# One unrolled phase for two attention layers and a dispatch, in place of two phases one after the other

## The chip, the cores and the metric

The kernel runs on one core of one Trainium2 chip. The metric is the device time of one execution in microseconds (us), as the median of several runs. PE is TensorE's matmul row, PEld its weight loads, DVE is VectorE, ACT is ScalarE, POOL is GpSimd, SP is SyncE. PEclk is the TensorE clock that was granted, as a share of full speed.

## The reference

The input is 256 images of 128 channels and 7x7 = 49 places. Six layers follow one another. The change touches the second and the third, and the gate of the fourth (cut from the reference):

```python
def _L1_conv_ref(x, gn_scale, gn_bias, wq, bq, wk, bk, wv, bv, wp, bp):
    h_ = group_norm(x, gn_scale, gn_bias)            # 32 groups of 4 channels, over channels and places
    q, k, v = conv1x1(h_, wq, bq), conv1x1(h_, wk, bk), conv1x1(h_, wv, bv)
    attn = jax.nn.softmax(einsum('bci,bcj->bij', q, k) * c ** -0.5, axis=-1)
    return x + conv1x1(einsum('bij,bcj->bci', attn, v), wp, bp)

def _L2_attn_ref(x):                                 # no weights: a normed token is query, key and value
    return einsum('bnm,bmd->bnd', jax.nn.softmax(einsum('bnd,bmd->bnm', x, x), axis=-1), x)

x = _L1_conv_ref(x, ...)
t = _to_tokens(x)                                    # (256 * 49 tokens) x 128
t = t + _L2_attn_ref(_ln_t(t))
t = t + _L2_ffn_ref(_ln_t(t), ...)                   # 8 experts, the 2 best of a token by its 8 scores
```

The expert layer is computed only for the two experts that a token chose. For that the kernel first sorts: it norms each token, computes its eight scores, picks two, and writes the token's row to a place in the region of each of the two experts in DRAM. This is the dispatch.

## The kernel before

`X` holds all of x on chip, 128 channels on partitions and 256 x 49 places along the row. Work goes by groups of 8 images (`GI`; a group is 392 columns, `T`), 32 groups (`NG`). Two images share the partitions of a score tile: one on rows 0 to 48, one on rows 64 to 112, so 113 rows (`R`). The program is a row of phases, each closed by a barrier of all engines: `heads_phase` (layer 0), `single_phase` (the convolution-style layer), `token_dispatch_phase` (token attention and the dispatch), `blocks_phase` (experts of layer 2), `combine_phase`, `scales_dispatch_phase` (layer 3's attention and its dispatch in one phase, 3 tiles a chunk), `blocks_phase`, `final_phase`.

Inside a phase each engine runs its own list in order, and counters (semaphores) hold it until another engine has done its part. The lists are staggered by hand: in step s an engine works on group s+4 for one operation, on s-1 for another, so that the chains of several groups overlap.

`single_phase` (name `conv_`): per group, DVE sums over places (`sums`), PE turns sums into means of four channels, DVE subtracts (`centre`), ACT squares, DVE sums (`squares`), PE, ACT `rstd`, DVE `norm` into `xn`; PE makes queries and keys, ACT writes them out with bias; PE makes values (`tokens`, with wv and wp multiplied into one matrix), DVE `v_out` copies them; PE scores, DVE maximum and subtraction (`shift`), ACT `expo`, DVE `total` and reciprocal, POOL multiplies (`probs`), PE transposes (`turn`), ACT writes that out in four pieces as a block-diagonal `pt` (`turned`), PE `values` over 113 rows, DVE `residual` into `X`. Steps 4 to 27 are a hardware loop.

`token_dispatch_phase` (name `d_`): the same attention without projections, `centre` as a matmul, all in unrolled code; `probs` on DVE. When the groups of a chunk of four 128-token tiles are through (25 chunks), `Dispatch` follows: PE `turn` (tile to rows, `xt`) and `logits`, DVE `stats`, ACT `rstd` and `norm` into `row`, DVE `scale`, `choose`, `count_up`, PE `positions`, DVE `place` and `weigh`, ACT `gate`, `names`, `second`. POOL does only `scatter`: for each tile two indirect DMAs (one for each chosen expert), 196 in all. SP loads and stores the expert weights that ACT and DVE split (`split_high`, `split_low`), and after `table` (DVE) writes pads behind each expert's rows.

Of the kernel before, what the change touches and what calls it, by code (L numbers as in the profile page):

```python
# [14 lines left out]
F32 = mybir.dt.float32  # L15
# [732 lines left out]
def single_phase(nc, sh, kind, weights=None):  # L748

    conv = kind == "conv"
    X, ident = sh.X, sh.ident
    LEAD = 4
    with ExitStack() as ctx:
        def sb(name, shape, dt=F32):
            return ctx.enter_context(nc.sbuf_tensor(f"{kind}_{name}", shape, dt))  # L760

        def ps(name, shape):
            return ctx.enter_context(nc.psum_tensor(f"{kind}_{name}", shape, F32))

        sem = ctx.enter_context(PhaseSemaphores(nc, kind))

        if conv:
            st, pjq, pjk = ps("st", [C, 512]), ps("pjq", [C, 512]), ps("pjk", [C, 512])
        else:
            cps = [ps(f"cen{i}", [C, 512]) for i in range(2)]  # L770
            st = ps("st", [C, 512])
        vps = ps("vps", [C, 4, C])
        sps, ptps, ops_ = ps("sps", [C, 512]), ps("ptps", [C, 512]), ps("ops", [C, 512])
        if conv:
            w, b_in = weights
            b_use = sb("b_use", [C, 4])
            csum, ssum = sb("csum", [C, GI]), sb("ssum", [C, GI])
            cen = [sb(f"cen{i}", [C, T]) for i in range(2)]
            qt, kt = sb("qt", [C, T]), sb("kt", [C, T])
            wvt, wvp = sb("wvt", [C, C]), sb("wvp", [C, C])  # L780
        sq = sb("sq", [C, T])
        rs = sb("rs", [C, GI if conv else T])
        xn = [sb(f"xn{i}", [C, GI, B1]) for i in range(2)]
        vt = [sb(f"vt{i}", [R, 4, C]) for i in range(4)]
        sc = sb("sc", [R, PAIRS, N])
        pr = [sb(f"pr{i}", [R, PAIRS, B1]) for i in range(2)]
        mx, sm = sb("mx", [R, PAIRS]), sb("sm", [R, PAIRS])
        rc = [sb(f"rc{i}", [R, PAIRS]) for i in range(2)]
        pt = [sb(f"pt{i}", [C, 2, 2, 2, N]) for i in range(2)]

        wready, bmm, zeroed = sem("weights_ready"), sem("bias_products"), sem("zeroed")
        csum_done, mean_done, cen_done, sq_done, ssum_done = sem("csum"), sem("mean"), sem("centred"), sem("squared"), sem("ssum")
        var_done, ln_done, rs_done, xn_done = sem("variance"), sem("logvar"), sem("rstd"), sem("normed")
        q_mm, k_mm, q_done, k_done, v_mm, v_done = sem("q_mm"), sem("k_mm"), sem("q_out"), sem("k_out"), sem("v_mm"), sem("v_out")
        wv_turned, wv_out, wvp_mm = sem("wv_turned"), sem("wv_out"), sem("wvp_mm")
        s_mm, max_done, sub_done, exp_done = sem("s_mm"), sem("maxed"), sem("shifted"), sem("exped")
        sum_done, rec_done, prob_done = sem("summed"), sem("recip"), sem("probs")
        t_mm, t_done, pv_mm, res_done = sem("t_mm"), sem("t_out"), sem("pv_mm"), sem("residual")

        block = ctx.enter_context(nc.Block())  # L800

        def images(ap):
            return ap.rearrange("c (b n) -> c b n", n=N)

        @block.tensor
        def _(pe):
            if conv:

                for m in range(3):
                    last = pe.matmul(sps[:, m:m + 1], w[:, m * C:(m + 1) * C], b_in[:, 5:6], start=(m == 0), stop=True,  # L810
                                     skip_group_check=True)
                last.then_inc(bmm, 1)

                pe.wait_ge(wready, 2)
                pe.matmul(sps[:, 3:4], w[:, 3 * C:4 * C], b_use[:, 2:3], start=True, stop=True,
                          skip_group_check=True).then_inc(bmm, 1)
                pe.transpose(ptps[:, 0:C], w[:, 2 * C:3 * C], ident[:, :]).then_inc(wv_turned, 1)
                pe.wait_ge(wv_out, 1)
                pe.matmul(ops_[:, 0:C], wvt[:, :], w[:, 3 * C:4 * C], start=True, stop=True).then_inc(wvp_mm, 1)
                pe.wait_ge(wready, 5)  # L820
            pe.wait_ge(zeroed, 6)

            def mean(at):
                g = at.g
                if not at.exists():
                    return
                if conv:
                    if due(g - 1):
                        pe.wait_ge(ln_done, g - 1)
                    pe.wait_ge(csum_done, g + 1)  # L830
                    pe.matmul(st[:, 0:GI], sh.group_w[:, :], csum[:, :], start=True, stop=True).then_inc(mean_done, 1)
                else:
                    if due(g - 1):
                        pe.wait_ge(xn_done, g - 1)
                    pe.matmul(cps[at.r % 2][:, 0:T], sh.centre_w[:, :], X[:, cols(g)], start=True, stop=True).then_inc(mean_done, 1)

            def var(at):
                g = at.g
                if not at.exists():
                    return  # L840
                if conv:
                    pe.wait_ge(cen_done, g + 2 if at.ahead(1).exists() else NG)
                    pe.wait_ge(ssum_done, g + 1)
                    pe.matmul(st[:, 0:GI], sh.group_w[:, :], ssum[:, :], start=True, stop=True).then_inc(var_done, 1)
                else:
                    pe.wait_ge(sq_done, g + 1)
                    if due(g):
                        pe.wait_ge(ln_done, g)
                    pe.matmul(st[:, 0:T], sh.mean_w[:, :], sq[:, :], start=True, stop=True).then_inc(var_done, 1)

            def queries(at):
                g = at.g
                if not at.exists() or not conv:
                    return
                x = xn[at.r % 2][:, :, 0:N]
                pe.wait_ge(xn_done, g + 1)
                if due(g):
                    pe.wait_ge(q_done, g)
                pe.matmul(pjq[:, 0:T], w[:, 0:C], x, start=True, stop=True).then_inc(q_mm, 1)
                if due(g):  # L860
                    pe.wait_ge(k_done, g)
                pe.matmul(pjk[:, 0:T], w[:, C:2 * C], x, start=True, stop=True).then_inc(k_mm, 1)

            def tokens(at):

                g = at.g
                if not at.exists():
                    return
                x = xn[at.r % 2]
                pe.wait_ge(xn_done, g + 1)  # L870
                if due(g):
                    pe.wait_ge(v_done, g)
                for mq in range(4):
                    two = x[:, 2 * mq:2 * mq + 2, :].rearrange("c b n -> c (b n)")
                    if conv:
                        last = pe.matmul(vps[:, mq, :], two, wvp[:, :], start=True, stop=True, skip_group_check=True)
                    else:
                        last = pe.transpose(vps[:, mq, :], two, ident[:, :])
                last.then_inc(v_mm, 1)

            def scores(at):
                g = at.g
                if not at.exists():
                    return
                if conv:
                    pe.wait_ge(k_done, g + 1)
                else:
                    pe.wait_ge(xn_done, g + 1)
                if due(g):
                    pe.wait_ge(sub_done, g)  # L890
                for p in range(PAIRS):
                    for m, rows in ((0, B1), (1, N)):
                        b = 4 * m + p
                        if conv:
                            q, k = qt[:, b * N:b * N + rows], kt[:, b * N:b * N + N]
                        else:
                            q, k = xn[at.r % 2][:, b, 0:rows], xn[at.r % 2][:, b, 0:N]
                        last = pe.matmul(sps[B1 * m:B1 * m + rows, p * N:(p + 1) * N], q, k, start=True, stop=True,
                                         skip_group_check=True)
                last.then_inc(s_mm, 1)  # L900

            def turn(at):
                g = at.g
                if not at.exists():
                    return
                pe.wait_ge(prob_done, g + 1)
                if due(g):
# [2021 lines left out]
```

## Time and profile before

| | |
|---|---|
| time, median of 3 runs (lowest, highest) | 2277.44 us (2272.39, 2285.70) |
| the profiled execution: its time, its span | 2277.56 us, 2275.8 us |
| share of the span busy: PE, PEld, DVE, ACT, POOL | 78%, 54%, 71%, 62%, 61% |
| mean granted TensorE clock | 0.894 |
| single_phase, first operation | 392.58 us |
| token_dispatch_phase, first operation | 562.79 us |
| blocks_phase of layer 2, first operation | 878.92 us |

The span runs from the first to the last instruction of the core. A busy share is a mean over phases that have different limits, so each phase is read by itself.

### The profile page before, as it was taken

The page shows a single profiled execution, that of the slowest core. Times are in us where ns is not written, and L with a number is a line of the kernel's source. Part 1 is how long each engine was busy: PE and PEld are TensorE (multiplying, and loading weights), DVE is VectorE, ACT ScalarE, POOL GpSimd, SP SyncE. Part 2 cuts the span into 40 slices and gives each one's busy share as a digit, 9 for nine tenths or more (in the row PEclk, how much of TensorE's full clock was granted, in tenths as well). Part 3 has the DMA queues.
Part 4 walks back from the last instruction along what each step waited for, and adds up shares of the span by engine and source line. Part 5 has one row for each costly group of instructions (what it writes and reads, how often), then busy time and mean ns, then how long its engine had stood idle before and what let it go on. Part 6 is the DMA issues. An engine that isn't in the chain of part 4 may idle for free. (4 is left out here: it accounts for less than half of the span.)

```text
span 2275.8 us, 52674 instructions
## 1 busy us (share of the span) xinstructions
PE 1781.9 (78%) x16257; PEld 1231.6 (54%) x16257; DVE 1615.1 (71%) x4634; ACT 1412.4 (62%) x3272; POOL 1399.3 (61%) x1482
## 2 busy tenths in 40 slices
PE   6999998898777743777764787787786299999974
PEld 3555554676566642555543354444444177777763
DVE  5888887787586652666654588888886378888864
ACT  5777775565666533555540698888885267777750
POOL 3555554010077773777776278888888557767765
PEclk9999998999898856999995898989997599999995
DMA  6000000000221124666546012111110367777748
GB/s 117 17 0 0 0 0 2 1 0 11 74 88 55 55 72 128 188 181 181 171 139 241 18 46 81 57 54 56 58 40 30 102 222 231 228 231 234 225 134 339
DMA packets 169828, 233.57 MB, mean 103 GB/s; under 512 B 60032, under 2 KB 131957, under 8 KB 162190
## 3 DMA queue, kind: packets, MB, share of 16 engines
q1 hardware_dynamic: 142446, 172.32, 25.1%
q0 software_dynamic: 26880, 52.27, 6.9%
q10 hardware_dynamic: 288, 6.42, 0.7%
q8 instruction: 99, 1.62, 0.3%
q14 instruction: 115, 0.94, 0.1%
HBM read 155.37 MB, written 79.23 MB: 103 GB/s over the span
## 5 line engine op out<-in xcount | busy, mean ns | idle before, releaser
L2684 POOL DMA_INDIRECT expert_out<-moe_yr,moe_to x448 | 493.1, 1101 | 255.0 <-DVE moe_yr L2663 132.9
L1558 POOL DMA_INDIRECT expert_rows<-d_row,d_pos x392 | 381.5, 973 | 190.5 <-issue 171.3
L2599 ACT ACTIVATE moe_ah<-moe_hps,moe_w 128x512 f32<-128x512 f32 (+1 forms) x336 | 230.4, 686 | 197.7 <-PE moe_hps L2549 193.9
L2640 DVE TENSOR_TENSOR moe_hl<-moe_ah,moe_hh 128x512 fp32r<-128x512 f32 (+1 forms) x336 | 235.5, 701 | 89.2 <-ACT moe_hh L2604 83.3
L1775 PE MATMUL scales_ptps<-ident,scales_pr 113*128 113x113 f32 x512 | 103.8, 307 | 95.5 <-DVE scales_sc L1873 64.1
L550 POOL TENSOR_TENSOR window_pr<-window_pr,window_rc 113x392 f32<-113x392 f32 x128 | 109.1, 852 | 106.8 <-DVE window_rc L494 106.8
L2547 PE MATMUL moe_hps<-moe_xh,moe_w 128*128 128x512 f32 (+1 forms) x336 | 138.4, 412 | 30.8 <-DMA moe_w<-moe_split 27.5
L2535 PE MATMUL moe_xps<-ident,moe_xb 128*128 128x128 f32 x448 | 73.1, 287 | 103.6 <-DMA moe_xb<-expert_rows 103.4
L1775 PEld LDWEIGHTS scales_ptps<-ident,scales_pr 113*128 113x128 f32 x512 | 65.7, 158 | 148.1 <-DVE scales_sc L1873 67.5
L2559 PE MATMUL moe_yps<-moe_hh,moe_w 128*128 128x512 f32 (+1 forms) x336 | 142.9, 425 | 0.9 <-DVE moe_hl L2640 0.9
L538 POOL TENSOR_TENSOR window_sc<-window_sc,window_mx 113x392 f32<-113x392 f32 x128 | 108.0, 844 | 50.2 <-DVE window_mx L468 49.2
L2549 PE MATMUL moe_hps<-moe_xh,moe_w 128*128 128x512 f32 (+1 forms) x336 | 134.7, 401 | 0.0
L2548 PE MATMUL moe_hps<-moe_xl,moe_w 128*128 128x512 f32 (+1 forms) x336 | 134.2, 400 | 0.0
L2560 PE MATMUL moe_yps<-moe_hl,moe_w 128*128 128x512 f32 (+1 forms) x336 | 133.0, 396 | 0.0
L2561 PE MATMUL moe_yps<-moe_hh,moe_w 128*128 128x512 f32 (+1 forms) x336 | 132.6, 395 | 0.0
L2535 PEld LDWEIGHTS moe_xps<-ident,moe_xb 128*128 128x128 f32 x448 | 53.7, 145 | 136.6 <-DMA moe_xb<-expert_rows 128.0
L657 ACT ACTIVATE window_pt<-window_ptps 128x452 f32<-128x452 f32 x128 | 69.8, 546 | 90.6 <-PE window_ptps L334 90.5
L2002 POOL TENSOR_TENSOR scales_pr<-scales_pr,scales_fac 113x416 f32<-113x416 f32 x128 | 114.2, 904 | 2.6 <-DVE scales_fac L1911 1.1
L2629 DVE TENSOR_TENSOR moe_xl<-moe_xps,moe_xh 128x512 fp32r<-128x512 f32 x112 | 76.4, 682 | 54.4 <-ACT moe_xh L2592 54.4
L1071 POOL TENSOR_TENSOR conv_pr<-conv_pr,conv_rc 113x196 f32<-113x196 f32 x32 | 16.5, 517 | 156.3 <-DVE conv_rc L1037 156.3
L2604 ACT ACTIVATE moe_hh<-moe_ah 128x512 fp32r<-128x512 f32 (+1 forms) x168 | 106.1, 632 | 5.3
L2638 DVE CAST moe_hh<-moe_ah 128x512 fp32r<-128x512 f32 (+1 forms) x168 | 86.3, 514 | 27.1 <-ACT moe_ah L2599 27.1
(287 smaller groups left out, 5203.9 us busy)
## 6 DMA issues: line engine op xcount, KB each, us to landing
moe_w<-moe_split SPq DMA_DIRECT2D x56, 1026.5 KB
moe_xb<-expert_rows SPq DMA_DIRECT2D x112, 264.0 KB, 3.0
moe_w<-moe_split SPq DMA_DIRECT2D x56, 449.5 KB
c_yy<-expert_out SPq DMA_DIRECT2D x28, 448.0 KB
final_yy<-expert_out SPq DMA_DIRECT2D x28, 448.0 KB
expert_out<-moe_yr,moe_to POOLq DMA_INDIRECT x448
X<-in_x SPq DMA_DIRECT2D x32, 196.0 KB, 2.8
expert_rows<-d_row,d_pos POOLq DMA_INDIRECT x392
```

Of the source, the lines that this page charges most:

```text
L1558: pool.indirect_dma_start(out=self.rows_dram, out_offset=bass.IndirectOffsetOnAxis(ap=self.pos[j][:, i, k:k + 1], axis=0), in_=self.row[j] ...
L1775: last = pe.transpose(ptps[:, hp * R:(hp + 1) * R], pr[at.r][p][:, 2 * hp:2 * hp + 2, :].rearrange("q h k -> q (h k)"), ident[0:R, 0:R])
L2535: last = pe.transpose(xps[:, t * C:(t + 1) * C], xb[b % NX][:, t, 0:C], ident[:, :])
L2547: pe.matmul(out, ww[:, W1H + k * P:W1H + (k + 1) * P], xh[j][:, :], start=True, stop=False)
L2548: pe.matmul(out, ww[:, W1H + k * P:W1H + (k + 1) * P], xl[j][:, :], start=False, stop=False)
L2549: pe.matmul(out, ww[:, W1L + k * P:W1L + (k + 1) * P], xh[j][:, :], start=False, stop=True).then_inc(h_mm, 1)
L2559: pe.matmul(out, ww[0:P, W2H + k * C:W2H + (k + 1) * C], high, start=(k == 0), stop=False)
L2560: pe.matmul(out, ww[0:P, W2H + k * C:W2H + (k + 1) * C], low, start=False, stop=False)
L2561: pe.matmul(out, ww[0:P, W2L + k * C:W2L + (k + 1) * C], high, start=False, stop=(k == K - 1)).then_inc(y_mm, 1)
L2599: act.activation(ah[n % NH][0:P, :], hps[n % 3][0:P, :], func, bias=bias(b, k)[0:P]).then_inc(h_done, 1)
L2640: dve.tensor_tensor(hl[n % NH][0:P, :], ah[n % NH][0:P, :], hh[n % NH][0:P, :].bitcast(F32), ALU.subtract).then_inc(hl_done, 1)
L2684: pool.indirect_dma_start(out=y_dram, out_offset=bass.IndirectOffsetOnAxis(ap=to[j][:, t:t + 1], axis=0), in_=yr[j][:, t, :], in_offset=No ...
```

## The change

`single_phase` and `token_dispatch_phase` become one phase, `conv_tokens_phase`, in which a group goes through the convolution-style layer, the token attention and, tile by tile, the dispatch. All steps are unrolled (46 steps, `LAST`). The orders of the engines' lists are written out. Beside the joining:

- the dispatch works by chunks of three tiles (33 chunks), rows and scores come from one matmul of 136 columns (`joint`), and the row buffers are four rings and not three;
- the convolution layer's `norm` moves from DVE to POOL, the token layer's `probs` and the expert weights' `split_low` from DVE to POOL, the convolution layer's `v_out` from DVE to ACT;
- the token layer's maximum and subtraction go away: `expo2` reads the scores from PSUM with a constant -64 added;
- `turned` writes two pieces and not four; most buffers are two to four deep; queries and keys share a PSUM bank, as do the score and transpose tiles, and the statistics, means and value products (`st`).

```diff
-def single_phase(nc, sh, kind, weights=None):
...
-            def body(s):
-                sums(s.ahead(4))
-                shift(s.ahead(1))
-                squares(s.ahead(3))
-                centre(s.ahead(4))
-                residual(s.ahead(-1))
-                total(s.ahead(1))
-                v_out(s.ahead(2))
-                norm(s.ahead(3))
...
-CHUNKS_D2 = chunks_of([4] * 24 + [2])
-CHUNKS_D3 = chunks_of([3] * 32 + [2])
+CHUNKS = chunks_of([3] * 32 + [2])
...
+        d = Dispatch(nc, sh, sb, sem, kind, e, wsplit, rows_dram, CHUNKS, [sorted_], sorted_[:, 3 * (C + EXPERTS):], joint=True, rings=4)
...
+            def var(g):
+                if not group(g):
+                    return
+                pe.wait_ge(cen_done, min(g + 2, NG))
+                after(pe, res_done, g - 4)
+                pe.wait_ge(ssum_done, g + 1)
+                pe.matmul(st[:, 0:GI], sh.group_w[:, :], ssum[g % 2][:, :], start=True, stop=True).then_inc(var_done, 1)
...
+            def turn2(g):
+                if not group(g):
+                    return
+                pe.wait_ge(prob2_done, g + 1)
...
+            for s in range(LAST):
+                var2(s - 9)
+                values(s - 8)
+                tokens(s - 7)
+                turn2(s - 10)
+                var(s - 3)
+                turn(s - 7)
+                queries(s - 4)
+                mean2(s - 8)
+                values2(s - 10)
+                scores2(s - 9)
+                ranks(s - 11)
+                mean(s - 1)
+                scores(s - 5)
+                keys(s - 4)
+                tokens2(s - 9)
+                turn_rows(s - 10)
             d.totals(pe)
...
+            for s in range(LAST):
+                if s == 4:
+                    d.prepare(dve)
+                sums(s)
+                if chunk(s - 11):
+                    d.stats(dve, s - 11)
+                residual(s - 8)
+                norm2(s - 9)
+                if chunk(s - 11):
+                    d.scale(dve, s - 11)
+                    d.choose(dve, s - 11)
+                    d.count_up(dve, s - 11)
+                total(s - 6)
+                squares(s - 2)
+                inverse(s - 6)
+                if chunk(s - 11):
+                    d.weigh(dve, s - 11)
+                    d.place(dve, s - 11)
+                residual2(s - 10)
+                centre(s - 1)
+                highest(s - 5)
+                total2(s - 9)
+                shift(s - 5)
+                inverse2(s - 9)
+            d.table(dve)
...
+            def norm(g):
+                if not group(g):
+                    return
+                after(pool, v_mm, g - 3)
+                pool.wait_ge(rs_done, g + 1)
+                pool.tensor_tensor(xn[g % 4][:, :, 0:N], images(cen[g % 4][:, :]), rs[g % 4][:, :][:, :, None].to_broadcast([C, GI, N]),
+                                   ALU.mult).then_inc(xn_done, 1)
...
+            for s in range(LAST):
+                norm(s - 1)
+                scatter(s - 10, 2)
+                probs(s - 4)
+                scatter(s - 9, 0)
+                probs2(s - 7)
+                scatter(s - 9, 1)
+                if group(s - 1) and s - 1 < EXPERTS:
+                    d.split_low(pool, s - 1)
+            d.all_sent(pool)
...
+                act.activation(pr2[g % 4][:, :, 0:N], sps2[0:R, 0:PAIRS * N].rearrange("t (p k) -> t p k", k=N), ACT.Exp,
+                               bias=low_exp[0:R, 0:1]).then_inc(exp2_done, 1)
...
+            for s in range(LAST):
+                v2_out(s - 12)
+                expo(s - 8)
+                rstd2(s - 11)
+                if chunk(s - 13):
+                    d.rstd(act, s - 13)
+                turned2(s - 12)
+                rstd(s - 5)
+                turned(s - 9)
+                rstd_out(s - 5)
+                if chunk(s - 13):
+                    act.wait_ge(d.scaled, s - 12)
+                    d.norm(act, s - 13)
+                    d.gate(act, s - 13)
+                q_out(s - 6)
+                if chunk(s - 13):
+                    d.names(act, s - 13)
+                    d.second(act, s - 13)
+                v_out(s - 9)
+                expo2(s - 11)
+                square2(s - 10)
+                square(s - 3)
+                k_out(s - 6)
+                if 4 <= s < 4 + EXPERTS:
+                    d.split_high(act, s - 4)
...
-            single_phase(nc, sh, "conv", conv)
-        token_dispatch_phase(nc, sh, "d2", MOE2, w2, rows_dram)
+            conv_tokens_phase(nc, sh, conv, "d2", MOE2, w2, rows_dram)
```

A name with a 2 behind it belongs to the token layer; the argument is the group (or, for the dispatch, the chunk) on which the call works in the list's step s.

## Rows read from the trace of the kernel before

**Rows 1.** Stretches: us, busy us (count) of PE, PEld, DVE, ACT, POOL, PEclk, DMA
```profile
410.00:555.00 145.00, 143.01 (x1265) 112.99 (x1266) 125.78 (x304) 87.53 (x302) 16.02 (x31) 1.00 0.00 1
600.00:700.00 100.00, 76.72 (x706) 61.61 (x705) 77.78 (x420) 67.50 (x237) 60.84 (x63) 0.98 0.28 90
790.00:820.00 30.00, 25.33 (x150) 23.72 (x151) 18.43 (x113) 12.47 (x55) 22.69 (x25) 0.50 0.16 53
...
1420.00:1720.00 300.00, 235.31 (x3152) 142.66 (x3152) 251.21 (x830) 257.78 (x663) 252.14 (x299) 0.91 0.16 52
```

**Rows 2.** Timeline of POOL in token_dispatch_phase: first and last of 196 scatters (start, us)
```profile
620.27 1.14 POOL L1558 DMA_INDIRECT expert_rows<-d_row,d_pos  x1 [61.89 <-issue]
...
867.86 0.95 POOL L1558 DMA_INDIRECT expert_rows<-d_row,d_pos  x1 [0.30 <-issue]
```

**Rows 3.** Groups by line, single_phase, 410 to 555: busy us, mean ns | idle before
```profile
L1010 DVE COPY conv_vt<-conv_vps 113x512 f32<-113x512 f32 x32 | 22.1, 692 | 21.2 <-PE conv_vps L876 21.2
...
L998 DVE TENSOR_TENSOR conv_xn<-conv_cen,conv_rs 128x392 f32<-128x392 f32 x31 | 17.4, 562 | 0.0
...
L1071 POOL TENSOR_TENSOR conv_pr<-conv_pr,conv_rc 113x196 f32<-113x196 f32 x31 | 16.0, 517 | 152.7 <-DVE conv_rc L1037 152.7
```

**Rows 4.** The same view, token_dispatch_phase, 600 to 700
```profile
L1313 PE MATMUL d_small<-d_wgc,X 128*128 128x8 f32 x88 | 10.5, 246 | 0.0
...
L2423 ACT ACTIVATE d_vt<-d_turn 113x512 f32<-113x512 f32 x14 | 8.5, 609 | 3.1 <-PE d_turn L2290 3.1
...
L2356 DVE TENSOR_TENSOR d_pr<-d_pr,d_rc 113x196 f32<-113x196 f32 x14 | 5.2, 372 | 0.5
L2339 DVE TENSOR_TENSOR d_sc<-d_sps,d_mx 113x196 f32<-113x196 f32 x14 | 5.1, 362 | 0.5
...
L1477 DVE TENSOR_TENSOR d_pick<-iota,d_idx 128x64 f32<-128x64 f32 x10 | 2.3, 226 | 0.3
...
L1465 DVE TENSOR_TENSOR d_gap<-d_top 128x4 f32<-128x4 f32 x10 | 1.7, 166 | 0.3
```

**Rows 5.** The same view, scales_dispatch_phase, 1420 to 1720
```profile
L1558 POOL DMA_INDIRECT expert_rows<-d_row,d_pos x117 | 115.1, 984 | 42.1 <-issue 33.2 <-ACT d_row L1401 8.7 <-DVE scales_sm L1882 0.2
...
L2011 POOL TENSOR_TENSOR scales_xn<-scales_xn,pos 128x392 f32<-128x392 f32 x19 | 19.7, 1035 | 0.5
...
L1477 DVE TENSOR_TENSOR d_pick<-iota,d_idx 128x48 f32<-128x48 f32 x20 | 16.5, 824 | 0.0
...
L1465 DVE TENSOR_TENSOR d_gap<-d_top 128x3 f32<-128x3 f32 x19 | 10.0, 527 | 0.7
```

**Rows 6.** One line by itself (min/median/max ns): a broadcast product on POOL in heads_phase
```profile
L538 POOL TENSOR_TENSOR window_sc<-window_sc,window_mx x128: 842/844/847, 27.6 to 381.9; 113x392 f32<-113x392 f32 x128
```

**Rows 7.** Timeline: first operation and first residual of each layer; a late chunk's dispatch
```profile
398.07 0.55 DVE L967 TENSOR_REDUCE conv_csum<-X 128x8 f32<-128x392 f32 x1
...
421.90 0.62 DVE L1045 SCALAR_TENSOR_TENSOR X<-conv_ops,conv_b_use,X 128x392 f32<-128x392 f32 x1
...
569.60 1.67 PE L2296 MATMUL d_cen<-X,centre_w 128*128 128x392 f32 x2 [6.20 <-DVE d_wgc L1415]
...
591.28 0.57 DVE L2343 TENSOR_TENSOR X<-d_ops,X 128x392 f32<-128x392 f32 x1 [1.20 <-PE d_ops L2271]
...
826.04 2.04 PE L1293 MATMUL d_xt<-d_wgc,X 128*128 128x128 f32 x8 [3.86 <-ACT d_row L1371]
...
831.40 0.22 DVE L1510 TENSOR_REDUCE d_pos<-d_at 128x8 uint32<-128x64 f32 x1
```

**Rows 8.** Timeline: the next phase's first operations, and the last scatter of scales_dispatch_phase
```profile
878.92 1.28 ACT L2584 ACT_TABLE_LOAD   x1 [32.03 <-PEq L101]
...
1799.41 0.96 POOL L1558 DMA_INDIRECT expert_rows<-d_row,d_pos  x1 [0.30 <-issue]
...
1813.08 1.28 ACT L2584 ACT_TABLE_LOAD   x1 [21.83 <-PEq L101]
```

More of the change, by code:

```diff
@@ L1687, in _ @@
             d.centre_gate(pe)
+            pe.wait_ge(d.ready, 6)
             pe.wait_ge(wready, 9)
@@ L2225, in images, with halves, chunk @@
             return ap.rearrange("c (b n) -> c b n", n=N)
+        def halves(bank, rows):
+            turned = bank[rows, 0:512]
+            return bass.AP(tensor=turned.tensor, offset=turned.offset, ap=[turned.ap[0], [B1, 2], [R, 2], [1, N]])
         def group(g):
             return 0 <= g < NG
-        def quads(step):
-            return [q for q, at in enumerate(turns) if at == step]
-        def chunks(step):
-            return [c for c, q in enumerate(d.last_quad) if turns[q] == step]
+        def chunk(c):
+            return 0 <= c < len(d.chunks)
         @block.sync
@@ new lines, in keys, with tokens @@
+            def keys(g):
+                if not group(g):
+                    return
+                pe.wait_ge(q_done, g + 1)
+                pe.matmul(pj[:, 0:T], w[:, C:2 * C], xn[g % 4][:, :, 0:N], start=True, stop=True).then_inc(k_mm, 1)
+            def tokens(g):
+                if not group(g):
+                    return
+                after(pe, v_done, g)
+                after(pe, v2_done, g - 2)
+                for mq in range(4):
+                    two = xn[g % 4][:, 2 * mq:2 * mq + 2, :].rearrange("c b n -> c (b n)")
+                    last = pe.matmul(vps[:, mq, :], two, wvp[:, :], start=True, stop=True, skip_group_check=True)
+                last.then_inc(v_mm, 1)
@@ L2250, in scores @@
+            def scores(g):
+                if not group(g):
+                    return
+                after(pe, sub_done, g)
+                after(pe, t_done, g - 1)
+                pe.wait_ge(k_done, g + 1)
                 for p in range(PAIRS):
@@ L2298, in _ @@
[L2298 to L2318 removed]
+                last.then_inc(t2_mm, 1)
@@ new lines, in values2 @@
+            def values2(g):
+                if not group(g):
+                    return
+                pe.wait_ge(ln2_done, min(g + 2, NG))
+                after(pe, res2_done, g)
+                pe.wait_ge(v2_done, g + 1)
+                pe.wait_ge(t2_done, g + 1)
+                for m in range(2):
+                    for q in range(2):
+                        mq = 2 * m + q
+                        last = pe.matmul(st2[:, mq * S2:(mq + 1) * S2], vt2[g % 4][:, mq, :],
+                                         pt2[g % 4][0:R, m, q].rearrange("k r n -> k (r n)"), start=True, stop=True, skip_group_check=True)
+                last.then_inc(pv2_mm, 1)
@@ new lines, in turn_rows, with ranks @@
+            def turn_rows(c):
+                if not chunk(c):
+                    return
+                if c == 0:
+                    pe.wait_ge(d.ready, 6)
+                after(pe, d.at_done, c)
+                pe.wait_ge(res2_done, min(c + 1, NG))
+                d.turn(pe, c)
+            def ranks(c):
+                if not chunk(c):
+                    return
+                pe.wait_ge(d.normed, c + 1)
+                d.positions(pe, c, c + 1)
+            for s in range(LAST):
[15 more added lines that the diff above has]
+                turn_rows(s - 10)
@@ new lines, in k_out, with v_out @@
+            def k_out(g):
+                if not group(g):
+                    return
+                act.wait_ge(k_mm, g + 1)
+                act.activation(kt[g % 2][:, :], pj[:, 0:T], ACT.Identity, bias=b_use[:, 1:2]).then_inc(k_done, 1)
+            def v_out(g):
+                if not group(g):
+                    return
+                after(act, pv_mm, g - 3)
+                act.wait_ge(v_mm, g + 1)
+                act.activation(vt[g % 4][:, :, :], vps[0:R, :, :], ACT.Copy).then_inc(v_done, 1)
@@ L2408, in turned @@
             def turned(g):
+                if not group(g):
+                    return
+                after(act, pv_mm, g - 3)
                 act.wait_ge(t_mm, g + 1)
-                if g >= 2:
-                    act.wait_ge(pv_mm, g - 1)
                 for r in range(2):
                     rows = slice(B1 * r, B1 * r + N)
-                    for m in range(2):
-                        last = act.activation(pt[g % 2][rows, m, :, r, :],
-                                              tps[rows, 0:2 * R].rearrange("k (q n) -> k q n", q=2)[:, :, B1 * m:B1 * m + N], ACT.Copy)
+                    last = act.activation(pt[g % 4][rows, :, :, r, :], halves(sps, rows), ACT.Copy)
@@ new lines, in turned2 @@
+            def turned2(g):
+                if not group(g):
+                    return
+                after(act, pv2_mm, g - 3)
+                act.wait_ge(t2_mm, g + 1)
+                for r in range(2):
+                    rows = slice(B1 * r, B1 * r + N)
+                    last = act.activation(pt2[g % 4][rows, :, :, r, :], halves(sps2, rows), ACT.Copy)
+                last.then_inc(t2_done, 1)
+            for s in range(LAST):
[23 more added lines that the diff above has]
+                    d.split_high(act, s - 4)
```

817 lines of the change are left out of this document (289 added, 528 removed).

## The prediction

> **What bounds the kernel now.** I read the page first for the phases' borders, then the stretches, then the groups by line inside each, then the timelines at the borders. The two phases that the change joins have opposite limits. In the convolution layer TensorE is busy for 143.0 of 145 us at full clock and POOL for 16.0 [rows 1]; 31 groups pass in that stretch [rows 3], so a group costs PE 4.61 us, and POOL sits idle for 152.7 us before its one product a group [rows 3]. In token attention POOL is what ends last: its first scatter starts at 620.27, its last ends at 867.86 + 0.95 = 868.81 [rows 2]. That is 248.5 us for 196 scatters, 1.268 us each, and no gap longer than the 0.30 us that each one has. In 600 to 700 PE is busy for 76.7 us and DVE for 77.8 [rows 1], mostly because POOL lets them through no faster. So the reader should see one phase that needs PE and leaves POOL idle, followed by one that needs POOL, and between them 620.27 - 398.07 = 222 us in which POOL scatters nothing.
>
> **The change, step by step.** A step of the new phase carries one group through each layer and three tiles through the dispatch.
>
> *PE.* The convolution group is 4.61 us. In 600 to 700, 14 groups passed [rows 4] with about three tiles each: 76.72 / 14 = 5.48 us. The separate score matmuls go (10.5 / 14 = 0.75 us [rows 4]). The sum is 9.3 us, or 10.1 if those 0.75 us lay under other matmuls already; I take 9.5.
>
> *POOL.* Six scatters, 6 x 1.268 = 7.61 us; two products of 113x196 at 0.517 each [rows 3], 1.03 us; and `norm`, which no row shows on POOL. Its bounds are 0.844 (the broadcast product in heads_phase, 113 partitions [rows 6]) and 1.035 (128x392 written into a strided tile [rows 5]); `norm` has the operands of the first and the output of the second, so 0.95. Sum: 9.59 us. The eight `split_low` stand before the first scatter, in steps when POOL has nothing else to do, so I cost them at nothing; if that cover is gone, each delays the first scatter by at most its own length.
>
> *DVE.* 125.78 / 31 + 77.78 / 14 = 9.62 us; minus `norm` 0.56 and `v_out` 0.69 [rows 3], `probs` 0.37, and maximum and subtraction at 0.36 each (the maximum is priced like the subtraction) [rows 4]: 7.3 us. Against that, two small DVE operations are longer where POOL computes beside them: `d_pick` 226 ns in rows 4 and 824 in rows 5, `d_gap` 166 and 527, together 0.96 us. There POOL computes for 252.1 - 115.1 = 137 of 300 us, 46%; here for 1.98 of 10 us, 20%: 0.4 us, at most 0.96. DVE gets 7.7 to 8.3.
>
> *ACT.* 87.53 / 31 + 67.50 / 14 = 7.64 us plus the moved `v_out` 0.61 [rows 4] = 8.3; halving the pieces of `turned` I count as no gain, which errs to the slow side.
>
> So POOL (9.6) and PE (9.5) are both near the bound, DVE and ACT under it. What moved to POOL lies on the bound; what left DVE gives nothing directly.
>
> The same product took 517 ns on POOL and 372 on DVE [rows 3, 4], a factor of 1.39. The Trainium skill, GPSIMD Engine Reference, section Engine selection, speaks against such a move: it puts elementwise work on VectorE and calls GpSimd about two times slower for two inputs. By that factor `norm` would take 2 x 0.562 = 1.12 us, and the sum below would be 23 x 0.17 = 4 us later; the rows decide, and I keep 0.95.
>
> *First scatter.* Three measured leads in a row give the early bound: first sum to end of first residual in the convolution layer, 422.52 - 398.07 = 24.45 us; first centring to first residual in token attention, 591.85 - 569.60 = 22.25; a late chunk from its turn to its places, 831.62 - 826.04 = 5.58 [rows 7]. With the setup up to 398.07 unchanged: 450.4. The late bound takes token attention's whole lead to its first scatter, 620.27 - 569.60 = 50.7 [rows 2, 7]: 473.2. The new lists place the first scatter ten steps after the first mean, and the steps grow as layers join; I take the middle, 462.
>
> *From there to the last.* By POOL's list, 9 `norm`, 6 `probs` and 2 `probs2` come before the first scatter. Left are 196 scatters (248.5), 23 norms (21.9; 19.4 to 23.8), and 26 + 30 products (56 x 0.517 = 29.0): 299.4 us. How much of its time can POOL work in such a mixture? scales_dispatch_phase has the same dispatch and a full POOL: 252.1 us busy and 33.2 us of issue between scatters [rows 5], 285.3 of 300 [rows 1], 0.951. There PE was busy for 78%; here it is nearly full too, so I take 0.94: 299.4 / 0.94 = 318.5, a full step 10.2 us. The last scatter ends at 462 + 318.5 = 780.5, before at 868.8: -88.3 us.
>
> *The end.* From the last scatter to the next phase it took 878.92 - 868.81 = 10.1 us, in scales_dispatch_phase 1813.08 - 1800.37 = 12.7 [rows 2, 8]. Before, `table` and the nine pads of SP ran under POOL's backlog; with POOL close behind the dispatch this cover shrinks: +2.6 us. The weights' 8 loads and 16 stores move to where the DMA engines are idle (share 0.00 in 410 to 555 [rows 1]): nothing.
>
> **New waits.** PE's `turn2` waits for `probs2`, which on POOL stands behind two scatters; behind `turn2` on PE wait `var`, `turn`, `queries` and ten more calls, so POOL's lateness reaches every engine. The bank `st` goes around once a step: `values`, DVE `residual`, PE `var`, ACT `rstd`, PE `mean`, DVE `centre`, next `values`. ACT waits for `d.scaled` before the dispatch's norm; behind it stands `q_out`, for which PE's `keys` waits.
>
> Sum: -88.3 + 2.6 = -85.7. The profiled execution took 2277.56, 0.12 from the median, so no correction: 2191.9, forecast **2192**. Its own range: first scatter 450.4, no loss, the low `norm`: 450.4 + 296.9 = 747.3, -121.5, 2156; first scatter 473.2 and POOL at work for 0.85 (0.951 less twice the 0.049 that scales_dispatch_phase loses): 473.2 + 352.2 = 825.4, -43.4 + 2.6, 2237.
>
> **Rivals.**
> *Two full lists hold each other up.* If `probs2` is late by its two scatters in each step, PE stands for up to 2.54 us. Full steps are those from PE's first `ranks` (11) to its last `mean` (32), 22. At half that price 28 us, at the whole 56: 2220 to 2248. For it: PE and POOL are 0.1 us apart, and in rows 5 POOL itself waited 8.7 us for ACT. Against it: 0.951 under almost the same lists [rows 1, 5].
>
> *The clock falls, and it ends slower.* In 790 to 820, where PE waits for POOL's pace, the granted clock is 0.50, its lower level of 1.2 GHz [rows 1]. At that level PE's 9.5 us become 19, and 22 steps of 19 in place of 10.2 add 194 us: 2386. It decides where the step gets longer than 10.2 + 85.7 / 22 = 14.1 us, a mean clock below 9.5 / 14.1 = 0.67. Against it: 1.00 where PE was busy for 99%, 0.91 where it was busy for 78% [rows 1]; here it is over 90%.
>
> *DVE is held up by POOL.* If each of its three two-input operations (`d_gap`, `d_pick`, `d_seen`) waits out a whole `norm`, DVE takes 7.3 + 2.85 = 10.2 us, no more than the step: inside the forecast's range.
> The Trainium skill, SBUF — State Buffer, section Who interferes with whom, says that a VectorE instruction with two SBUF inputs and a GpSimd one that reads SBUF exclude each other for a whole instruction. By that rule the three waits are the ceiling, and the lengthened rows 5 agree.
>
> *The joining gains nothing.* The shared banks make the layers take turns, and a step takes the 14.1 us of the sum above: 2277.
>
> **Chances.** Forecast 0.70, held-up lists 0.17, still less loss than my best bound 0.05, no gain 0.03, slower clock 0.05. Beyond 0.5% (11 us, what a measurement here tells from no change): faster 0.92, same 0.03, slower 0.05. The range for 8 in 10 covers the forecast's bounds and most of the held-up case: 2155 to 2245.
>
> **What would show it.** Right: first scatter at 450 to 473 us; scatters at 0.30 us gaps with products between; POOL's busy time plus that issue above 90% of a mid-phase stretch; PE above 90% at a clock over 0.9; next phase at about 793. Wrong: PE idle before `turn2` for microseconds a step, a clock near 0.5 in mid-phase, a step above 12 us, or a first scatter far outside that span.

## The result, and the profile after

The changed kernel takes 2158.68 us (2157.49 to 2158.98, 4 runs); the kernel before, measured beside it, 2276.58 (2272.39 to 2285.70, 4 runs). The ratio on record is 0.9472, its 95% interval 0.9456 to 0.9488; the two medians alone give 0.9482. The profiled execution took 2157.49 us with a span of 2155.7, so 120.1 us less span than before. The forecast was 2192: the sign, the place and the engine were right, and about 34 us of the gain (120.1 in place of 85.7) were not foreseen.

First the borders of the new phase: POOL's first and last of its 196 scatters, then the first operation of the phase behind it, and that phase's counterpart after the second dispatch.

```profile
452.38 1.14 POOL L1148 DMA_INDIRECT expert_rows<-d_row,d_pos  x1 [1.52 <-issue]
...
744.47 0.96 POOL L1148 DMA_INDIRECT expert_rows<-d_row,d_pos  x1 [0.30 <-issue]
758.16 1.28 ACT L2491 ACT_TABLE_LOAD   x1 [21.99 <-PEq L101]
...
1693.31 1.28 ACT L2491 ACT_TABLE_LOAD   x1 [22.09 <-PEq L101]
```

The last scatter ends at 744.47 + 0.96 = 745.43, before at 868.81 [rows 2]: 123.4 us sooner. The next phase starts 758.16 - 745.43 = 12.7 us later (10.1 before), so it is 120.8 us sooner than before [rows 8]. The table load after the second dispatch is 1813.08 - 1693.31 = 119.8 us sooner: what lies between did not change by more than 1 us. The whole gain is in the joined phase.

Now the stretches inside it: length, busy time of PE, PEld, DVE, ACT, POOL with counts, PEclk, DMA.

```profile
452.00:480.00 28.00, 27.63 (x267) 22.86 (x266) 23.76 (x115) 25.03 (x81) 22.98 (x26) 1.00 0.13 43
480.00:680.00 200.00, 193.38 (x1850) 159.53 (x1849) 161.68 (x782) 172.50 (x550) 166.43 (x193) 1.00 0.14 46
680.00:720.00 40.00, 31.32 (x279) 24.56 (x277) 26.27 (x148) 27.80 (x90) 31.86 (x37) 0.92 0.16 51
720.00:746.00 26.00, 6.46 (x35) 5.21 (x35) 14.42 (x83) 7.17 (x31) 19.48 (x21) 0.50 0.37 109
```

Before, one layer filled PE and left POOL idle and the other did the reverse [rows 1]; now PE is busy for 97% of the 200 us in the middle, at a granted clock of 1.00, and POOL for 83%. Which of the two sets the step can't be read from that row. It can from POOL's list itself, one step of it (all tiles of the joined phase have names in `d_`; L1148 is `scatter`, L2204 `norm`, L2212 `probs`, L2219 `probs2`):

```profile
597.60 0.84 POOL L2204 TENSOR_TENSOR d_xn<-d_cen,d_rs 128x392 f32<-128x392 f32 x1
598.61 1.01 POOL L1148 DMA_INDIRECT expert_rows<-d_row,d_pos  x1 [0.17 <-issue]
599.92 0.96 POOL L1148 DMA_INDIRECT expert_rows<-d_row,d_pos  x1 [0.30 <-ACT d_row L991]
600.90 0.52 POOL L2212 TENSOR_TENSOR d_pr<-d_pr,d_rc 113x196 f32<-113x196 f32 x1
601.59 1.01 POOL L1148 DMA_INDIRECT expert_rows<-d_row,d_pos  x1 [0.16 <-issue]
602.90 0.96 POOL L1148 DMA_INDIRECT expert_rows<-d_row,d_pos  x1 [0.30 <-issue]
603.89 0.52 POOL L2219 TENSOR_TENSOR d_pr<-d_pr,d_rc 113x196 f32<-113x196 f32 x1
604.57 1.01 POOL L1148 DMA_INDIRECT expert_rows<-d_row,d_pos  x1 [0.16 <-issue]
605.89 0.96 POOL L1148 DMA_INDIRECT expert_rows<-d_row,d_pos  x1 [0.30 <-issue]
606.88 0.85 POOL L2204 TENSOR_TENSOR d_xn<-d_cen,d_rs 128x392 f32<-128x392 f32 x1
```

From one `norm` to the next it is 9.28 us, and no gap in it is longer than the 0.30 that a scatter has behind another. From the first scatter to the last that pattern has two exceptions, a gap of 0.39 us at 458.16 and this one, for which the profile names no cause:

```profile
629.07 0.97 POOL L1148 DMA_INDIRECT expert_rows<-d_row,d_pos  x1 [1.62 <-issue]
```

The rows also show what an arithmetic instruction costs in such a list. A scatter that follows another directly starts 1.265 us after it (0.96 + 0.30). With a product between, the starts are 1.67 us apart (599.92 to 601.59), and the scatter after it is 0.05 longer: the product costs 1.67 + 1.31 - 2 x 1.265 = 0.45 us, less than its 0.52, because the scatter behind it shows a gap of 0.16 and not 0.30. In the same way `norm` costs 2.00 + 1.31 - 2.53 = 0.78 to 0.79 us.

The groups by line in 480 to 680 (busy us, mean ns of one, idle before), and two of the longest waits of that stretch (total us, times, longest):

```profile
L1148 POOL DMA_INDIRECT expert_rows<-d_row,d_pos x129 | 126.8, 983 | 31.6 <-issue 25.8 <-ACT d_row L991 5.8
L2204 POOL TENSOR_TENSOR d_xn<-d_cen,d_rs 128x392 f32<-128x392 f32 x20 | 16.9, 846 | 0.9 <-ACT d_rs L2259 0.3
L1067 DVE TENSOR_TENSOR d_pick<-iota,d_idx 128x48 f32<-128x48 f32 x21 | 5.3, 253 | 0.7
L1055 DVE TENSOR_TENSOR d_gap<-d_top 128x3 f32<-128x3 f32 x21 | 3.8, 181 | 0.9 <-DVE d_top L1047 0.2
```

```profile
PE d_sps_ps L2008 <- POOL d_pr L2219: 6.6, 21, 1.6
...
POOL expert_rows L1148 <- ACT d_row L991: 5.8, 19, 0.3
```

POOL's named wait in front of scatters is ACT's `second`, never above 0.3 us, so it lies inside the gap that a scatter has anyway; in front of `norm` one wait of 0.3 us for ACT's `rstd_out` is named. PE's wait before `turn2` for `probs2` is there, 0.3 us a step.

### The profile page after: what moved, and what is told of

It reads as the page before. It is cut to its first block and busy times, and to the rows that moved or that the text cites. A ratio compares the mean times of both kernels' runs of the same rounds, so it can differ in the third digit from the quotient of the medians.

```text
span 2155.7 us, 52223 instructions
## 1 busy us (share of the span) xinstructions
PE 1733.1 (80%) x16077; PEld 1198.8 (56%) x16077; DVE 1551.9 (72%) x4519; ACT 1427.1 (66%) x3231; POOL 1456.7 (68%) x1570
## 5 line engine op out<-in xcount | busy, mean ns | idle before, releaser
L1148 POOL DMA_INDIRECT expert_rows<-d_row,d_pos x392 | 384.0, 980 | 117.7 <-issue 94.2
L2454 PEld LDWEIGHTS moe_hps<-moe_xh,moe_w 128*128 128x128 f32 (+1 forms) x336 | 61.4, 183 | 68.1 <-DMA moe_w<-moe_split 47.1
```

The lines of the kernel that those rows point to most:

```text
L1148: pool.indirect_dma_start(out=self.rows_dram, out_offset=bass.IndirectOffsetOnAxis(ap=self.pos[j][:, i, k:k + 1], axis=0), in_=self.row[j] ...
L2454: pe.matmul(out, ww[:, W1H + k * P:W1H + (k + 1) * P], xh[j][:, :], start=True, stop=False)
```

## The experiments

Three theories for the 9.28 us step. A: POOL's list, without a hole, sets it. B: PE's list sets it and POOL follows. C: the two lists hold each other up through `turn2`, so that each delay comes back in the next step. Each variant starts from the changed kernel; its time is set beside 2158.68. A few microseconds of that difference mean nothing: the kernel before took 2280.28 to 2284.21 us beside the variants, against 2276.58 beside the changed kernel, and the part behind the joined phase, whose code is the same in all of them, took 1397.5 us in the changed kernel's profile and up to 1407.9 in a variant's. So each variant also gets what its profile shows inside the joined phase: the step, the stretch from first to last scatter (293.05 us in the changed kernel) and the start of the next phase (758.16).

**`norm` on VectorE.**
```diff
 # POOL
-                norm(s - 1)
                 scatter(s - 10, 2)
 # VectorE
                 inverse(s - 6)
+                norm(s - 3)
```


> The convolution's norm goes back to VectorE, after inverse; all else as in the changed kernel. Theory A (POOL's list without a hole sets the 9.28 us step): norm costs that list 0.79 us a step (two scatter starts that are 3.31 us apart around it, where two bare intervals take 2.52), so POOL's list falls to 8.49 and PE, at 193.38 us of work in 21.55 steps = 8.97, becomes the limit: 22 x 0.3 = 7 us less, up to 23 x 0.79 = 18 where POOL's backlog at the end goes too: 2141 to 2152. Theory B (PE's list sets the step, POOL follows): no gain, 2156 to 2162. VectorE gets 7.5 + 0.56 = 8.1 us a step and is no limit in either.


2148.33 us (2146.66 to 2150.01); the ratio to the kernel before is 0.9405, interval 0.9390 to 0.9421, which does not meet that of the changed kernel. The step is 8.84 us (two `probs2` five steps apart start at 561.29 and 605.49), the scatters take 280.91 us, and the next phase starts at 746.40, 11.8 us sooner. The stretch of this kernel, columns as above, then a scatter beside VectorE's `norm`:

```profile
480.00:680.00 200.00, 198.61 (x1958) 166.51 (x1956) 176.62 (x855) 182.40 (x583) 162.24 (x183) 1.00 0.15 48
...
565.74 0.54 DVE L2142 TENSOR_TENSOR d_xn<-d_cen,d_rs 128x392 f32<-128x392 f32 x1
565.82 1.29 POOL L1148 DMA_INDIRECT expert_rows<-d_row,d_pos  x1 [0.30 <-issue]
```

PE is now busy for 99%. A holds, and no complete version of this study is clearly faster: the move of `norm` to POOL cost 10 to 12 us. POOL is not simply idle for the rest of the 8.84, though: in most steps the scatter that starts just after VectorE's `norm` takes 1.29 us or a little more in place of 0.96, and that makes POOL's list 8.49 + 0.33 = 8.82 long. That PE's list is 8.84 rests on the last run below, where POOL has time to spare and the step stays.

**One product more on POOL.**
```diff
                 scatter(s - 9, 1)
+                extra(s - 7)     # a 113x196 product of two constant tiles
```


> One more 113x196 product a step on POOL, into a tile that nobody reads, behind the last scatter of each step. A: each of the 30 that come after the first scatter adds its own 0.50 us to a list without a hole: +15, 2174. B: POOL has 9.28 - 8.92 = 0.36 us of slack a step, so 22 x 0.14 = 3 us at most in the full steps: 2159 to 2162. Theory C (the two lists hold each other up through turn2): as in A or more, since each lateness returns through PE: 2174 to 2190.


2175.65 us (2171.03 to 2177.05), +17.0; the next phase starts at 771.85, 13.7 later. Two `norm`s six steps apart:

```profile
566.30 0.86 POOL L2208 TENSOR_TENSOR d_xn<-d_cen,d_rs 128x392 f32<-128x392 f32 x1
...
624.78 0.85 POOL L2208 TENSOR_TENSOR d_xn<-d_cen,d_rs 128x392 f32<-128x392 f32 x1
```

The step is 58.48 / 6 = 9.75, +0.47. A further piece of POOL's list counts with all that it costs there, so B falls; C's lower end, 2174, is met as well.

**PE computes `mean2` twice.**
```diff
+                pe.matmul(cps2[:, 0:T], sh.centre_w[:, :], X[:, cols(g)], start=True, stop=True)
                 pe.matmul(cps2[:, 0:T], ..., start=True, stop=True).then_inc(mean2_done, 1)
```


> PE computes mean2 twice, +0.82 us of PE work a step. A: PE's list gets 8.97 + 0.82 = 9.79 us and passes POOL's 9.28, so only the excess of 0.5 us counts: 22 x 0.5 = 11, and some of it is taken back from POOL's backlog of the last steps: 2160 to 2170. B: the whole 0.82 counts in 22 to 26 steps: +18 to +21, 2177 to 2180. C: the same 18 or more.


2169.30 us (2164.04 to 2170.47), +10.6, a ratio of 0.9489 whose interval, 0.9469 to 0.9508, meets that of the changed kernel; the next phase starts at 765.44, 7.3 later. The step settles it, at 9.50 us, with PE busy throughout:

```profile
480.00:680.00 200.00, 199.11 (x1864) 163.74 (x1863) 158.05 (x771) 172.21 (x545) 163.35 (x189) 1.00 0.14 45
```

With PE's list of 8.84 from the run with `norm` on VectorE, and 0.66 us from `mean2`'s start to the next matmul's, this is 8.84 + 0.66: PE passes POOL and only the excess counts, as A said.

**Half of the token layer's values left out on PE.**
```diff
-                for mq in range(4):      # tokens2
+                for mq in range(2):
-                for m in range(2):       # values2
+                for m in range(1):
```


> PE leaves out half of the token layer's transposes of values and half of its value products (the output is not the reference's): 0.8 us of PE work less a step, POOL unchanged. A (POOL's list sets the step): no gain, 2156 to 2161, step 9.28, PE idle for about 1 us a step. B (PE's list sets it): the step falls by 0.36 at least, to POOL's own 8.92: 22 x 0.36 = 8 or more: 2135 to 2151.


2158.31 us (2154.07 to 2160.21): no gain, step 9.30, scatters in 293.26 us. PE's waiting before `turn2` grew instead:

```profile
PE d_sps_ps L2008 <- POOL d_pr L2219: 16.9, 22, 2.1
```

**The same, and `norm` on VectorE.** The two edits above together.


> The same work left out on PE, and norm on VectorE. A: PE's list is 8.2 us, POOL's 8.49, so POOL sets the step again and the whole 23 x 0.79 = 18 us comes: 2138 to 2143; the difference to norm on VectorE alone is what PE's limit had kept back there. B: as with the work left out alone, 2135 to 2151, and norm adds nothing.


2140.01 us (2138.56 to 2144.91), -18.7. The step is 8.52, POOL's list without `norm` (9.28 - 0.79 = 8.49). The four corners settle it between A and B: less work on PE alone shortens the scatters' stretch by 0, on POOL alone by 12.1 us, on both by 19.2 (273.87). In the changed kernel POOL's list sets the step with 9.28 us, and PE's stands at 8.84, 0.44 us behind it. One more limit, just as long as POOL's list, comes to light in the run with `probs2` late.

**Maximum and subtraction put back** into the token layer, on VectorE.
```diff
+                highest2(s - 9)
                 residual2(s - 10)
+                shift2(s - 9)
```


> The token layer gets its maximum and subtraction back on VectorE, 0.73 us a step, between the score products and the exponential. A: VectorE has 161.68 / 21.55 = 7.5 us of work a step, 8.2 then, under 9.28: 2157 to 2163. If the way from scores2 to probs2 is on the ring that sets the step, each step gets up to 0.7 us longer: +15, 2174.


2160.50 us (2159.07 to 2167.34), step 9.30, next phase at 758.52: the removed operations, 0.73 us a step, were worth nothing that can be told here.

**Three buffers for the rows in place of four.**
```diff
-        d = Dispatch(..., joint=True, rings=4)
+        d = Dispatch(..., joint=True, rings=3)
```


> The changed kernel with three instead of four buffers for a chunk's rows. If the fourth buffer is what keeps POOL's list without a hole (the analog with three stood at 0.951): ScalarE waits for scatters, POOL for ScalarE, a loss up to that of the analog, 5% of 293 us = 15: 2165 to 2174. If a row is free again soon enough (a chunk is written and scattered within about two steps): 2156 to 2161.


2162.12 us (2156.77 to 2162.76), ratio 0.9470 (0.9454 to 0.9487) against 0.9472; the next phase starts at 756.85. The fourth buffer is not what closes POOL's list.

**The token layer 32 steps later**, behind the convolution, in the new phase with its new operations.
```diff
 # on every engine, for the token layer and the dispatch
-                var2(s - 9)
+                var2(s - 41)
 # tokens(g) on PE
-                after(pe, v2_done, g - 2)
```


> The new phase with its new lists and operations, but token attention and its dispatch are put 32 steps later, so that they begin where the convolution layer ends. If the gain is the overlap: the convolution runs at PE's 4.6 us a group, the first scatter comes at about 600, then POOL takes 6 x 1.268 + 0.45 = 8.05 us a step for 32.7 steps, last scatter about 863, next phase about 876, as before the change: 2265 to 2285. If a good part of the gain is the lighter operations (no maximum, joint products, larger copies): 2200 to 2250.


2282.29 us (2277.07 to 2296.08); the ratio to the kernel before is 1.0001, 0.9981 to 1.0021. The whole gain goes when the overlap goes, and the next phase starts at 882.18 (878.92 before the change). The first scatter and the two stretches of this run:

```profile
599.34 1.14 POOL L1148 DMA_INDIRECT expert_rows<-d_row,d_pos  x1 [6.48 <-DVE d_pos L1100]
```

```profile
440.00:560.00 120.00, 113.50 (x1036) 91.61 (x1036) 74.96 (x190) 83.97 (x219) 32.29 (x50) 1.00 0.02 8
700.00:860.00 160.00, 111.27 (x804) 80.89 (x804) 94.52 (x567) 95.79 (x320) 122.20 (x135) 0.82 0.15 50
```

First PE is full and POOL idle, then POOL is full and PE waits, at a clock of 0.82: the picture of [rows 1] with the new operations.

**`probs2` behind its two scatters.**
```diff
                 scatter(s - 9, 0)
-                probs2(s - 7)
                 scatter(s - 9, 1)
+                probs2(s - 7)
```


> On POOL the token layer's probs2 goes behind the second chunk's next two scatters, so PE's turn2 can get its operand 2.6 us later. A: POOL's list keeps its length, PE falls behind once by at most 2.6 us and not in each step: 2157 to 2163. C (the two lists hold each other up, the rival of the prediction): PE stands for up to 2.6 us more in each of 22 steps, 8.97 + 2.6 - 9.28 = 2.3 us longer: +25 to +50, 2184 to 2209.


2235.84 us (2233.11 to 2237.15), +77, of it 74.9 in the phase (next phase at 833.04): A's 2.6 us once is wrong, and so is C's upper bound. What C describes is a ring: a way from POOL through other engines back to POOL. One turn of it in this run, first POOL, then ACT:

```profile
598.61 0.96 POOL L1148 DMA_INDIRECT expert_rows<-d_row,d_pos  x1 [0.30 <-issue]
599.60 0.52 POOL L2219 TENSOR_TENSOR d_pr<-d_pr,d_rc 113x196 f32<-113x196 f32 x1
602.59 0.84 POOL L2204 TENSOR_TENSOR d_xn<-d_cen,d_rs 128x392 f32<-128x392 f32 x1 [2.47 <-ACT d_rs L2259]
```

```profile
600.69 0.67 ACT L2338 ACTIVATE d_pt<-d_sps_ps 49x196 f32<-49x196 f32 x2 [1.73 <-PE d_sps_ps L2008]
601.39 0.27 ACT L2253 ACTIVATE d_rs<-d_st_ps,eps 128x8 f32<-128x8 f32 x1
601.55 0.66 ACT L2297 ACTIVATE d_pt<-d_sps_ps 49x196 f32<-49x196 f32 x2
602.24 0.21 ACT L2259 ACTIVATE d_rs<-d_rs 128x8 f32<-128x8 f32 x1
```

`probs2` ends at 600.12. PE's `turn2`, ACT's `turned2`, `rstd`, `turned` and `rstd_out` follow, and `norm` can start at 602.59, 2.47 us later, while POOL stands. The step is 11.82 us, 2.54 more. POOL stands like this in all 23 steps that still have a `norm`, and in the 7 after them for 1.7 to 3.3 us before the first scatter of a chunk, for its places: the last scatter ends 74 us later (818.7 + 0.96). In the changed kernel the same way takes the same time:

```profile
594.61 0.52 POOL L2219 TENSOR_TENSOR d_pr<-d_pr,d_rc 113x196 f32<-113x196 f32 x1
...
597.24 0.21 ACT L2259 ACTIVATE d_rs<-d_rs 128x8 f32<-128x8 f32 x1
```

From `probs2`'s end at 595.13 to `norm` at 597.60 it is 2.47 us too, but there two scatters fill it. ScalarE's `rstd_out` ends at 597.45, 0.15 us before `norm` starts; in the late run, where `norm` waits for it, that distance is 0.14. So the ring has no slack in the changed kernel: it and POOL's list are equally long to about 0.01 us, and no run separates them (`norm` on VectorE removes both). By this, less work on POOL between `probs2` and `norm` alone would gain nothing; that was not tried.

**Both: `probs2` late and `norm` on VectorE.** If `norm` were the only place where the ring closes, this would undo the loss.


> probs2 behind its two scatters as in the late run, and norm on VectorE. Theory R (the ring of the late run closes through norm alone: probs2, PE's turn2, ScalarE's turned2, rstd, turned and rstd_out, then POOL's norm, 2.47 us, while POOL stands): without norm on POOL nothing there waits for ScalarE's rstd_out, POOL stays ahead, and the time is that of norm on VectorE with probs2 early: 2146 to 2156. Theory S (the ring closes through the dispatch: turn2, values2, residual2, the next chunk's places, scatter): probs2's place costs as before, some +75: 2205 to 2235.


2212.89 us (2211.48 to 2216.16): theory R falls, S holds in kind, though the price against `norm` on VectorE is 61 us in the phase (807.15 against 746.40) and 65 in the whole time, not 75. In this run POOL, which no longer waits for `rstd_out`, waits before the first scatter of each chunk: in 480 to 680 13 times for rows (ACT's `second`, 2.0 to 2.4 us) and 5 times for places. One of the latter, with VectorE's `norm` beside POOL's product:

```profile
598.46 0.53 POOL L2220 TENSOR_TENSOR d_pr<-d_pr,d_rc 113x196 f32<-113x196 f32 x1
...
601.41 0.57 DVE L2142 TENSOR_TENSOR d_xn<-d_cen,d_rs 128x392 f32<-128x392 f32 x1 [0.91 <-ACT d_rs L2259]
601.45 0.90 POOL L2213 TENSOR_TENSOR d_pr<-d_pr,d_rc 113x196 f32<-113x196 f32 x1
605.23 1.00 POOL L1148 DMA_INDIRECT expert_rows<-d_row,d_pos  x1 [2.88 <-DVE d_pos L1100]
```

```profile
599.05 0.41 PE L2008 MATMUL d_sps_ps<-ident,d_pr 113*128 113x113 f32 x2 [1.65 <-POOL d_pr L2220]
...
604.30 0.17 PE L926 MATMUL d_sorted_ps<-d_base,d_ones 128*128 128x24 bf16 x1
```

PE's `ranks` stands in its list behind `turn2`, and ACT's `second` in its own behind `turned2`, which waits for `turn2`; from `probs2` to the places it is 6.2 us (598.99 to 605.23), more than the 2.5 us of scatters and the 0.9 of the product that POOL has left by then. So there are two rings through `turn2`, one back to `norm` and one to the next chunk's scatters, and the place of `probs2`, with one pair of scatters behind it, keeps both covered.

**`norm` and the convolution's `probs` on VectorE.**
```diff
                 inverse(s - 6)
+                norm(s - 3)
+                probs(s - 6)
```


> norm and the convolution's probs both on VectorE. If with norm alone there the step (8.84 us) is PE's list, taking 0.45 us a step more off POOL gives nothing in the full steps, and only what is left of POOL's backlog at the end: 2142 to 2149. If POOL still sets it: 23 x 0.45 = 10 less, 2136 to 2140. If VectorE (176.62 us in 22.6 steps = 7.8, then 8.2) holds PE up by the longer way to turn: 2150 or more.


2149.61 us (2146.69 to 2154.17), step 8.85; the next phase starts at 744.52, 1.9 us sooner than with `norm` alone, and the rest of the kernel took 9 us more in this profile. POOL now has time to spare once a step:

```profile
565.13 1.34 POOL L1148 DMA_INDIRECT expert_rows<-d_row,d_pos  x1 [0.30 <-issue]
567.21 0.96 POOL L1148 DMA_INDIRECT expert_rows<-d_row,d_pos  x1 [0.73 <-issue]
```

That gap is 0.43 us longer than the usual 0.30, and PE is busy for 198.29 of 200 us: PE's list sets this step.

## Why the prediction was right, and where its numbers were off

The time lies inside the stated range, but only 4 us from its lower end of 2155, because the two large errors, in the first scatter and in the stretch behind it, both went to the slow side.

*The bound.* Right: PE and POOL close together, POOL ahead. POOL's step was forecast at 9.59 and is 9.28; PE's at 9.5 and is 8.84, below its lower bound of 9.3. That bound came from PE's busy time in a stretch where it waited for POOL [rows 4]; why a group costs less where PE runs through was not tried. DVE was forecast at 7.7 to 8.3 a step (its first sum comes to 9.61, not 9.62, which changes nothing) and has 161.68 / 21.55 = 7.5; ACT 8.3 and has 8.0.

*First scatter.* 452.38, inside 450.4 to 473.2 and 9.6 us before the value taken. The measured leads in a row were the better estimate; the middle between the bounds was a guess.

*From first to last scatter.* This step failed in size: 318.5 us forecast, 293.05 measured, 25.4 less. About 7.4 of it are the pieces: 0.79 for `norm` in place of 0.95 (23 of them) and 0.45 for a product in place of 0.517 (56). The other 18 are the occupancy, 0.94 forecast and practically 1 measured (299.4 - 7.4 = 292.0 of 293.05; the gap at 629.07 is most of the rest). The 0.951 of scales_dispatch_phase [rows 1, 5] was taken as a property of a full list beside a full PE. It belongs to that phase: its POOL waits 8.7 us for ACT in 5 waits of up to 2.0, beyond the gaps; here the same wait never exceeds 0.3 and stays inside them.

*The end.* +2.6 forecast, 10.1 to 12.7 measured: right.

*Nothing for the removed operations* on VectorE: right, by the run that puts two of them back.

*The rival of two full lists* did not come true, but the mechanism is real and was priced too low: 28 to 56 us, where the run with `probs2` late lost 77, 75 of them in the phase. The price of a step was right at its upper end (2.54 us). What was too low is the number of steps: the prediction counted PE's standing in 22 full ones, and POOL stands in 30, nearly every step that carries scatters. That the changed kernel escapes it, with no slack in the ring, the prediction did not work out.

*The clock* stayed at 1.00 in the middle. It fell at the end of the phase, and from 720 on, where PE was busy for 6.46 of 26 us, it was 0.50.

*DVE beside POOL.* `d_pick` takes 253 ns and `d_gap` 181, against 208 and 164 with `norm` off POOL: 0.06 us a step for the two, where 0.4 was allowed. It is the order that makes them longer and not `norm` on POOL as such: with the maximum put back `norm` is on POOL too, and `d_pick` takes 208. In the changed kernel a scatter starts during 16 of the 21 `d_pick`, and these alone take 0.26 to 0.28 us; of the `d_gap` a single one, at 633.07, met a product on POOL and took 0.53. The other long ones of [rows 5] do not appear, since they seldom meet a product here. Two other runs show what a meeting does. With `probs2` late and `norm` on VectorE, `norm`, which reads two tiles in SBUF, overlapped a product on POOL 27 times, and each time one of the two was held until the other was done: 22 products took 0.75 to 0.91 us in place of 0.52 and ended 0.37 after `norm`, and 5 `norm`s took 0.72 to 1.00 in place of 0.54 and ended 0.42 to 0.44 after the product. A scatter that starts up to 0.08 us after `norm` does is held as well, and ends 0.83 us after `norm`'s end (566.28 and 567.11 in the first run above). The rule of the Trainium skill (SBUF — State Buffer, Who interferes with whom) that the two kinds of instruction exclude each other agrees with that.

*Elementwise work on POOL.* The same `norm` took 846 ns on POOL and 539 on VectorE, 1.57 times; the page GPSIMD Engine Reference, Engine selection, of the Trainium skill says about two. Its factor was too high here, but its advice was right, and the forecast passed it over: `norm` on VectorE is 10 to 12 us faster, since POOL sets the step.

*What stays open:* why PE's list is 0.66 us a step shorter than forecast, what POOL's gap of 1.62 us at 629.07 is, and what orders the first steps up to 452 us.

## What to carry to other kernels

When two phases with opposite bounds are joined, add up the list of each engine for one step and look for the list without a hole; a product between two scatters costs less than its own time, and an occupancy is not carried over from another phase without the waits that made it. A step with two nearly full lists then hangs on the order of a single instruction: count the time from what it releases back to what its own engine needs next, on every way back, and keep at least that much work behind it. A list without a hole does not show that such a ring is just as long: look at how long before its use the last operand was ready. After such a join, work on the engine that sets the step is the first to give back, even to an engine that looks busy.

## What was not expected of the hardware

The gap in front of an indirect scatter on POOL is 0.30 us after another scatter and 0.16 to 0.17 after an arithmetic instruction, which itself starts 0.02 to 0.03 us after a scatter; so a 0.52 us product in such a list lengthens it by 0.45. POOL kept this up for 293 us with one gap of 1.62, in the middle 200 us beside a PE at 97%, with its products at 525 ns (517 in the quiet phase before [rows 3]).

A scatter shows a hold in its own length and not as a gap: beside VectorE's `norm` it took 1.29 us in place of 0.96, with the usual 0.30 in front of it.
